# Attention over normalized images on one core: ten query sets that stay within a batch, four first tiles and two last ones transposed by TensorE, and the moves of a set shared by three DMA queues

## The chip, the cores and the metric

The kernel runs on one core of one Trainium2 chip. The metric is the device time in microseconds (us) of one execution; it is given as the median of several runs. An execution is also profiled once, and the trace of that execution is what the rows below are read from.

## What is computed

Four images x[b] of 128 channels by 1024 positions pass through one block of group norm, attention and projection, with a residual:

```
h = group_norm(x, 8 groups) * gn_w + gn_b
q = qw h + qb ; k = kw h + kb ; v = vw h + vb        # 128 x 1024 each
attn = softmax(q^T k / sqrt(128), axis=-1)           # 1024 x 1024 for each image
out = x + pw (v attn^T) + pb
```

All of it is float32.

## The kernel before

**Tiles and sets.** The 1024 queries of each of the 4 images are cut into 8 tiles of 128, so the program has 32 steps, numbered c = 0 to 31; b = c // 8 is the image ("batch") and i = c % 8 the tile in it. Step c makes the scores of tile c. The q and k weights are multiplied into one matrix beforehand (`g` is that product applied to h), and v carries the projection already. Scores are accurate products of float32 numbers split in a high and a low part (`h_hi`, `h_lo`, `g_hi`, `g_lo`): six matmuls of 512 columns a tile.

**What happens to one tile.** TensorE (PE) writes the scores into PSUM (`scores`). VectorE (DVE) copies them out with a bias and takes the row minimum (`drain_scores`, s_sb). ScalarE (ACT) takes the exponential and its sum (`exponentials`). The product with v needs the probabilities with keys on the partitions, that is transposed. For most tiles this is done in two parts: DVE transposes blocks of 32 x 32 (`transpose_blocks`, blocks), and DMA then moves the blocks from one group of 32 partitions to another (pT<-blocks). A set of four tiles is moved together, by 16 DMAs ("pieces") of 32 partitions x 4 KB: one for each source group a and destination group j. The first and the last two tiles are transposed by PE instead (`transpose_probs`, eight matmuls a tile into PSUM, copied out half by ACT and half by DVE, `copy_pair`). These are called direct.

**Sets.** `SETS = (2, 4, 4, 4, 4, 4, 4, 4, 2)`: set 0 and set 8 are direct, sets 1 to 7 are moved. Set 2 is tiles 6 to 9, so it lies half in image 0 and half in image 1; sets 4 and 6 cross an image in the same way. A set's product with v is done in units, one a tile, of eight matmul passes of 256 columns (`value_unit`). In a set within one image the units go by source groups: the first two need groups a = 0 and 1, that is the first 8 pieces, the last two the rest. In a set that crosses an image, each unit needs all 16 pieces.

**Order of work.** Every engine has one hand-written program, a loop over c, in order; engines wait for one another on semaphores. PE in step c does the scores of c, then the extra work of an image (`value_tiles`, `project_g` for the next image in steps with i = 6, 1, statistics), then the value unit of c - LAG, with LAG = 8. SP issues all DMAs but a few: `move_set(n)` waits until DVE has transposed the last tile of set n, which it does in step FIRST[n+1] (FIRST[n] is the first tile of set n), then issues the 16 pieces. GpSimd (POOL) computes the low part of h for the next image (`split_h`, i = 4), which the last matmul pass of `project_g` in steps 6, 14 and 22 reads, and adds the residual of finished sets. ACT also sends the inverse softmax sums of a set to a DRAM buffer (`copy_rows`, row_store), from where SP spreads them over all partitions (`spread_rows`, rden_bc<-row_store), so that DVE can divide (`divide`).

Of the kernel before, what the change touches and what calls it, by code (L numbers as in the profile page):

```python
# [22 lines left out]
LAG = 8  # L23


def build(nc, x, vectors, weights, out):
# [22 lines left out]
    with ExitStack() as ctx:  # L49
# [14 lines left out]
        def is_direct(c):  # L64
            return c < SETS[0] or c >= DIRECT

        def direct_number(c):
            return c if c < SETS[0] else c - DIRECT + SETS[0]

        def columns(n):  # L70

            return slice(P * FIRST[n], P * (FIRST[n] + SETS[n]))

        def last_batch(n):
            return (FIRST[n] + SETS[n] - 1) // CH

        def crosses(n):

            return FIRST[n] // CH != last_batch(n)

        def divided_in(c):

            for n in range(LS - 2):
                last = FIRST[n] + SETS[n] - 1
                if c == (FIRST_UNIT_STEPS[last] + 3 if n == 0 else last + LAG + 1):
                    return n
            return None
# [43 lines left out]
        pair_T = sb("pair_T", [P, KT, 2, P])  # L131
# [7 lines left out]
        sums = [ACC[:, n % 2, 0:P * SETS[n]] for n in range(LS)] + [S[:, 1, 0:PN]]  # L139
        last_sums = [ACC[:, (LS - 1) % 2, 0:UW], ACC[:, LS % 2, 0:UW]]  # L140
# [19 lines left out]
        MOVED = 16 * NQ  # L160
# [5 lines left out]
        normed_ready, last_normed, out_ready, tail_out_ready, stored = map(sem, ("normed_ready", "last_normed", "out_ready", "tail_out_ready", "stored"))  # L166
        tp_psum = sem("tp_psum")
        pair_ready = [sem(f"pair_ready{f}") for f in range(HALVES)]

        xb_flat = xb[:, :, :].rearrange("p b n -> p (b n)")  # L170
# [7 lines left out]

        block = ctx.enter_context(nc.Block())

        @block.sync
        def _(sp):
            def move_set(n):
                sp.wait_ge(blocks_ready, FIRST[n + 1] - SETS[0])
                if n > 2:
                    sp.wait_ge(part_done, FIRST[n - 1])
                for a in range(NQ):
                    for j in range(NQ):
                        sp.dma_start(moved_view(n)[Q * j:Q * (j + 1), a].rearrange("p t n -> p (t n)"),  # L189
                                     blocks_view(n)[Q * a:Q * (a + 1), j].rearrange("p t c q -> p (t c q)"))\  # L190
                          .then_inc(moved[n % 2][a], 16)
# [8 lines left out]
            def store_set(n):  # L200
                if n < SPREAD_BY_DMA:
                    sp.wait_ge(out_ready, n + 1)
                else:
                    sp.wait_ge(tail_out_ready, 2 if n == LS else 3)
                at = P * FIRST[n]
                while at < P * (FIRST[n] + SETS[n]):
                    b, first = at // N, at % N
                    width = min(N, first + P * (FIRST[n] + SETS[n]) - at) - first
                    sp.dma_start(out[b, :, first:first + width], xb[:, b, first:first + width]).then_inc(stored, 16)
                    at += width  # L210
# [20 lines left out]
            sp.wait_ge(stored, 16 * (NS + sum(crosses(n) for n in range(NS))))  # L231

        @block.tensor
        def _(pe):
            def group_deviations(b):
# [3 lines left out]
                if b > 1:  # L239
# [28 lines left out]
            def project_g(b, f):  # L268
# [598 lines left out]
```

## Time and profile before

| | us |
|---|---|
| median of 3 runs | 144.14 (143.91 to 144.76) |
| the profiled execution, its own time | 144.62 |
| its span, first to last instruction | 142.6 |
| PE busy | 130.1 |
| DVE busy | 99.5 |
| ACT busy | 64.9 |
| POOL busy | 26.1 |

The busy time of an engine counts computing instructions alone; the issuing of DMAs, as on SP, is not in it. The granted TensorE clock was full through the whole span.

### The profile page before, as it was taken

The numbers are of one execution on the slowest core, as the hardware profiler recorded it, in microseconds if no ns is written. First come the engines' busy times: TensorE is split into PE (matmuls) and PEld (weight loads), VectorE is DVE, ScalarE is ACT, GpSimd is POOL, SyncE is SP. The second block draws the span as 40 slices with busy tenths as digits, with TensorE's granted clock in tenths as the row PEclk, the third lists the DMA queues.
The fourth block names the chain that finished last, engine by engine and source line by source line (L and its number), as shares of the span: only waits on it lengthen the run. The fifth ranks groups of instructions, "written<-read, shape, count | busy, mean of one in ns | idle before, by whom it ended". The sixth has DMA issues, their size and how long they took to land.

```text
span 142.6 us, 2014 instructions
## 1 busy us (share of the span) xinstructions
PE 130.1 (91%) x647; PEld 109.4 (77%) x647; DVE 99.5 (70%) x172; ACT 64.9 (46%) x112; POOL 26.1 (18%) x33
## 2 busy tenths in 40 slices
PE   5999999997779999799999995999999969999990
PEld 5997878865558887688888883888888847988880
DVE  0577779989998679679697789366977893521222
ACT  4053789564566653544436845054543333512000
POOL 5043050930202061100050323000030030003000
PEclk9999999999999999999999999999999999999999
DMA  4950000005996799499824997899509987979211
GB/s 147 306 210 0 0 5 0 27 12 115 214 205 168 171 211 203 118 205 210 195 93 92 202 209 200 202 204 210 162 0 205 209 195 202 205 161 223 78 37 74
DMA packets 9565, 20.98 MB, mean 147 GB/s; under 512 B 2362, under 2 KB 4052, under 8 KB 9556
## 3 DMA queue, kind: packets, MB, share of 16 engines
q1 hardware_dynamic: 8816, 20.59, 59.3%
q10 hardware_dynamic: 740, 0.28, 0.7%
q8 instruction: 5, 0.08, 0.2%
q14 instruction: 4, 0.03, 0.1%
HBM read 4.07 MB, written 2.11 MB: 43 GB/s over the span
## 4 chain that ended last, share of the span: by engine, by line
PE 56%; SPq 19%; DVE 11%; issue 6%; DMA 5%; POOL 0%; DVEq 0%; POOLq 0%
PE ACC L377 20%; SPq L189 19%; PE S L322 6%; DMA pT<-blocks 5%; PE S L326 5%; PE S L323 5%; PE S L266 5%; DVE blocks L665 4%; DVE s_sb L656 4%; PE A L302 3%; PE ACC L350 2%; PE S L350 2%; PE A L404 1%; PE ACC L404 1%; DVE bn L581 1%
## 5 line engine op out<-in xcount | busy, mean ns | idle before, releaser
L377 PE MATMUL ACC<-pT,v 128*128 128x256 f32 x224 | 52.8, 381 | 4.1 <-DMA pT<-blocks 4.1
L656 DVE TENSOR_SCALAR_CACHE_REDUCE s_sb<-S,row_term 128x1024 f32<-128x1024 f32 x32 | 41.0, 1281 | 20.7 <-PE S L326 20.2
L377 PEld LDWEIGHTS ACC<-pT,v 128*128 128x128 f32 x224 | 41.2, 190 | 10.9 <-issue 5.6
L502 ACT ACTIVATE s_sb<-s_sb,rowmin 128x1024 f32<-128x1024 f32 x32 | 36.8, 1151 | 20.9 <-DVE s_sb L656 19.9
L665 DVE STREAM_TRANSPOSE blocks<-s_sb 128x1024 f32<-128x1024 f32 x28 | 34.7, 1240 | 0.0
L322 PE MATMUL S<-h_hi,g_hi 128*128 128x512 f32 x64 | 30.2, 472 | 0.3 <-issue 0.3
L323 PE MATMUL S<-h_lo,g_hi 128*128 128x512 f32 x64 | 25.2, 393 | 0.0
L326 PE MATMUL S<-h_hi,g_lo 128*128 128x512 f32 x64 | 19.9, 392 | 0.0
L810 POOL TENSOR_TENSOR xb<-rden_bc,xb 128x512 f32<-128x512 f32 (+1 forms) x7 | 8.4, 1194 | 53.0 <-DVE rden_bc L685 45.5
L326 PEld LDWEIGHTS S<-h_hi,g_lo 128*128 128x128 f32 x64 | 12.0, 188 | 2.8
L322 PEld LDWEIGHTS S<-h_hi,g_hi 128*128 128x128 f32 x64 | 12.1, 189 | 2.5 <-issue 0.4
L494 ACT COPY v<-A 128x384 f32<-128x384 f32 (+1 forms) x12 | 5.3, 443 | 18.8 <-PE A L302 18.8
L323 PEld LDWEIGHTS S<-h_lo,g_hi 128*128 128x128 f32 x64 | 12.1, 189 | 2.0
L302 PEld LDWEIGHTS A<-wpv,h 128*128 128x128 f32 x64 | 8.4, 191 | 3.7 <-issue 2.6
L302 PE MATMUL A<-wpv,h 128*128 128x129 f32 x64 | 9.5, 281 | 1.3 <-DVE g_lo L630 1.1
L797 POOL TENSOR_TENSOR h_lo<-h,h_hi 128x1024 fp32r<-128x1024 f32 x3 | 7.2, 2398 | 17.8 <-ACT h L472 17.8
L266 PE MATMUL S<-ident 128*128 128x128 f32 x38 | 7.9, 363 | 1.6 <-POOL ident L814 1.6
L482 ACT ACTIVATE g_hi<-A,wpv 128x512 fp32r<-128x512 f32 x7 | 4.8, 689 | 9.4 <-PE A L284 9.4
L266 PEld LDWEIGHTS S<-ident 128*128 128x128 f32 x38 | 6.9, 265 | 1.6 <-POOL ident L814 1.6
L788 POOL TENSOR_TENSOR rstd<-gvar,minus_half 128x1 f32<-128x1 f32 x4 | 2.2, 552 | 30.6 <-DVE gvar L603 30.6
L581 DVE BATCH_NORM_STATS2 bn<-x_sb 128x6 f32<-128x512 f32 x8 | 5.3, 683 | 2.9 <-DMA x_sb<-x 2.9
L467 ACT ACTIVATE h_hi<-x_sb,gshift,gscale 128x1024 fp32r<-128x1024 f32 (+1 forms) x5 | 5.2, 1067 | 2.1 <-DVE gshift L614 1.6
(90 smaller groups left out, 103.4 us busy)
## 6 DMA issues: line engine op xcount, KB each, us to landing
pT<-blocks SPq DMA_DIRECT2D x112, 128.0 KB, 2.4
rden_bc<-row_store SPq DMA_DIRECT2D x6, 256.0 KB, 3.6
x_sb<-x SPq DMA_DIRECT2D x1, 1024.0 KB, 6.0
out<-xb SPq DMA_DIRECT2D x8, 128.0 KB, 2.8
out<-xb SPq DMA_DIRECT2D x4, 256.0 KB, 3.2
x_sb<-x SPq DMA_DIRECT2D x2, 256.0 KB, 3.0
x_sb<-x SPq DMA_DIRECT2D x1, 512.0 KB, 3.9
w_in<-weights ACTq DMA_DIRECT2D x2, 128.0 KB, 3.5
```

The lines of the kernel that those rows point to most:

```text
L189: sp.dma_start(moved_view(n)[Q * j:Q * (j + 1), a].rearrange("p t n -> p (t n)"), blocks_view(n)[Q * a:Q * (a + 1), j].rearrange("p t c q ...
L266: pe.matmul(S[:, 0, BANK:BANK + P], ident[:, :], ident[:, :], start=True, stop=True)
L302: last = pe.matmul(A1[:, PW1 * u:PW1 * (u + 1)], h[:, P * t:P * (t + 1)], wpv[:, 0:PW1], start=True, stop=True)
L322: pe.matmul(S[:, c % 2, ks], g_hi[:, qs], h_hi[:, b % 2, ks], start=True, stop=False)
L323: pe.matmul(S[:, c % 2, ks], g_hi[:, qs], h_lo[:, b % 2, ks], start=False, stop=False)
L326: last = pe.matmul(S[:, c % 2, ks], g_lo[:, qs], h_hi[:, b % 2, ks], start=False, stop=True)
L377: last = pe.matmul(to, v[:, b % 3, t, :], probs[:, :, t, :], start=(t == 0), stop=(t == KT - 1))
L502: act.activation(s_sb[:, c % 3, :], s_sb[:, c % 3, :], ACT.Exp, bias=rowmin[:, c % CH:c % CH + 1], scale=-1.0, accum_out=den[:, n % 2, k:k ...
L656: dve.tensor_scalar(s_sb[:, c % 3, :], S[:, c % 2, :], row_term[:, b % 2, i:i + 1], None, ALU.add, ALU.min, accum_out=rowmin[:, i:i + 1]). ...
L665: dve.transpose(blocks_view(n)[:, :, :, k, :].rearrange("p j t q -> p t j q"), s_sb[:, c % 3, :].rearrange("p (t j q) -> p t j q", t=KT, j ...
L797: pool.tensor_tensor(h_lo[:, b % 2, :], h[:, :], h_hi[:, b % 2, :].bitcast(F32), ALU.subtract).then_inc(h_lo_ready, 1)
L810: pool.tensor_tensor(xs, rden_bc[:, n % 2, 0:P * SETS[n]], xs, ALU.add).then_inc(out_ready, 1)
```

## The change

- `SETS` becomes `(2, 2, 4, 4, 4, 4, 4, 4, 2, 2)`. Sets 0, 1 and 9 are direct (tiles 0 to 3 and 30, 31), sets 2 to 7 are moved sets of four tiles, and set 8 (tiles 28, 29) is a moved set of two. No set crosses an image. So two more tiles than before, 2 and 3, are transposed by PE.
- LAG becomes 7, and the units of tiles 0 to 3 run in steps 4 to 7; before, those of tiles 0 and 1 ran in steps 4 and 5, and those of tiles 2 and 3 in steps 10 and 11.
- Of the 16 pieces of sets 2 to 7, SP issues the 12 with j = 0 to 2 and POOL the 4 with j = 3, in step FIRST[n+1], ahead of `split_h`. Of the 16 pieces of set 8, which are half as long, SP issues 8 and ACT 8.
- The inverse sums are turned at i = 3 and 5 and copied by ACT at i = 4 and 6; SP's program takes `spread_rows(2)` ahead of `move_set(3)`, and after that each `spread_rows(n)` stands between `move_set(n)` and `move_set(n + 1)`.
- The last sets are finished without the halves that the set before last had.

The diff, cut to its core:

```diff
-SETS = (2, 4, 4, 4, 4, 4, 4, 4, 2)
-
-FIRST_UNIT_STEPS = (4, 5)
-LAG = 8
+SETS = (2, 2, 4, 4, 4, 4, 4, 4, 2, 2)
+PAIRS = 4
+
+FIRST_UNIT_STEPS = (4, 5, 6, 7)
+FIRST_DIVIDED_STEPS = (7, 9)
+LAG = 7
...
+        def move_piece(engine, n, a, j, counted):
+
+            engine.dma_start(moved_view(n)[Q * j:Q * (j + 1), a].rearrange("p t n -> p (t n)"),
+                             blocks_view(n)[Q * a:Q * (a + 1), j].rearrange("p t c q -> p (t c q)"))\
+                  .then_inc(counted[n % 2][a], 16)
...
             def move_set(n):
-                sp.wait_ge(blocks_ready, FIRST[n + 1] - SETS[0])
-                if n > 2:
+                sp.wait_ge(blocks_ready, FIRST[n + 1] - PAIRS)
+                if n > 3:
                     sp.wait_ge(part_done, FIRST[n - 1])
                 for a in range(NQ):
-                    for j in range(NQ):
...
+                    for j in range(NQ - 1 if n < LS - 1 else NQ // 2):
+                        move_piece(sp, n, a, j, moved)
...
             spread_rows(0)
-            move_set(1)
             spread_rows(1)
+            move_set(2)
             store_set(0)
-            for n in range(2, LS):
+            store_set(1)
+            spread_rows(2)
+            for n in range(3, LS):
                 move_set(n)
+                if n > 3:
+                    store_set(n - 2)
                 if n < SPREAD_BY_DMA:
                     spread_rows(n)
-                if n > 2:
-                    store_set(n - 2)
...
             def moved_unit(n, u):
-                b, part, half = (FIRST[n] + u) // CH, u // 2, u % 2
+                b, size = FIRST[n] // CH, SETS[n]
+                a0, width, half = (2 * (u // 2), 2, u % 2) if size == GC else (0, NQ, u)
...
+                    for a in range(a0, a0 + width):
+                        pe.wait_ge(moved[n % 2][a], MOVED * (n // 2) + (16 if n == LS - 1 else 0))
+                        if n < LS - 1:
+                            pe.wait_ge(keys_moved[n % 2][a], 16 * (n // 2))
...
-                if c - 1 in FIRST[1:LS]:
-                    turn_rden(FIRST.index(c - 1) - 1)
+                if i == 3 and (b == 0 or c > CH):
+                    turn_rden(2 * b if b > 0 else 0)
+                if i == 5:
+                    turn_rden(2 * b + 1)
...
             value_unit(STEPS - LAG)
+            value_unit(STEPS - LAG + 1)
             transpose_probs(STEPS - 1)
...
+            def move_last_set():
+                n = LS - 1
+                act.wait_ge(blocks_ready, DIRECT - PAIRS)
+                act.wait_ge(part_done, FIRST[n - 1])
+                for a in range(NQ):
+                    for j in range(NQ // 2, NQ):
+                        move_piece(act, n, a, j, moved)
...
                 exponentials(c)
+                if c == DIRECT:
+                    move_last_set()
...
+            def move_last_keys(n):
+                pool.wait_ge(blocks_ready, FIRST[n + 1] - PAIRS)
+                if n > 3:
+                    pool.wait_ge(part_done, FIRST[n - 1])
+                for a in range(NQ):
+                    move_piece(pool, n, a, NQ - 1, keys_moved)
...
                     add_bias((1, 3, 6, 7).index(c))
+                if c in FIRST[3:LS]:
+                    move_last_keys(FIRST.index(c) - 1)
                 if i == 4 and b < L:
                     split_h(b + 1)
```

Where this moves instructions is seen in the order of each engine's program.

First GpSimd, from the residual of set 0 (step 8 before, step 7 after) to that of set 2 (step 14 before, step 15 after). rstd and gscale are the group norm of the next image, h_lo is `split_h`. Before:

```order
L810 TENSOR_TENSOR xb<-rden_bc,xb 128x256
L788 TENSOR_TENSOR rstd<-gvar,minus_half 128x1
L790 TENSOR_TENSOR gscale<-rstd,cols 128x1
L797 TENSOR_TENSOR h_lo<-h,h_hi 128x1024
L810 TENSOR_TENSOR xb<-rden_bc,xb 128x512
```

After:

```order
L813 TENSOR_TENSOR xb<-rden_bc,xb 128x256
L174 DMA pT<-blocks 32x1024 x4
L813 TENSOR_TENSOR xb<-rden_bc,xb 128x256
L791 TENSOR_TENSOR rstd<-gvar,minus_half 128x1
L793 TENSOR_TENSOR gscale<-rstd,cols 128x1
L174 DMA pT<-blocks 32x1024 x4
L800 TENSOR_TENSOR h_lo<-h,h_hi 128x1024
L813 TENSOR_TENSOR xb<-rden_bc,xb 128x512
```

Four DMAs of set 2 stand in step 8 now, and four of set 3 in step 12, right ahead of h_lo; the same stands in step 20.

Second SP, from the loads of x on (rden_bc<-row_store is `spread_rows`, out<-xb a store). Before:

```order
L217 DMA x_sb<-x 128x2x1024
L197 DMA rden_bc<-row_store 128x256
L189 DMA pT<-blocks 32x1024 x16
L197 DMA rden_bc<-row_store 128x512
L209 DMA out<-xb 128x256
L189 DMA pT<-blocks 32x1024 x16
L197 DMA rden_bc<-row_store 128x512
```

After:

```order
L210 DMA x_sb<-x 128x2x1024
L194 DMA rden_bc<-row_store 128x256 x2
L174 DMA pT<-blocks 32x1024 x12
L203 DMA out<-xb 128x256 x2
L194 DMA rden_bc<-row_store 128x512
L174 DMA pT<-blocks 32x1024 x12
L194 DMA rden_bc<-row_store 128x512
```

A train has 12 pieces in place of 16, and the sums of set 2 are spread ahead of the moves of set 3.

Third PE, from the projection of g for image 1 in step 6 through step 7 (S is the scores, A<-wpv,h the value tiles, A<-ident,rden the turned sums). Before:

```order
L284 MATMUL A<-h_lo,wa_hi 128x512
L322 MATMUL S<-h_hi,g_hi 128x512
L323 MATMUL S<-h_lo,g_hi 128x512
L322 MATMUL S<-h_hi,g_hi 128x512
L323 MATMUL S<-h_lo,g_hi 128x512
L326 MATMUL S<-h_hi,g_lo 128x512 x2
L334 MATMUL A<-ident,rden 4x128
L302 MATMUL A<-wpv,h 128x129 x3
```

After:

```order
L283 MATMUL A<-h_lo,wa_hi 128x512
L358 MATMUL ACC<-pair_T,v 128x256 x4
L321 MATMUL S<-h_hi,g_hi 128x512
L322 MATMUL S<-h_lo,g_hi 128x512
L321 MATMUL S<-h_hi,g_hi 128x512
L322 MATMUL S<-h_lo,g_hi 128x512
L325 MATMUL S<-h_hi,g_lo 128x512 x2
L301 MATMUL A<-wpv,h 128x129 x3
L358 MATMUL ACC<-pair_T,v 128x256 x4
```

The units of tiles 2 and 3 (ACC<-pair_T,v) have come into steps 6 and 7, in which PE had none before.

## Rows read from the trace of the kernel before

**Rows 1.** The page: busy time, the chain by engine, and the group of drains.

```profile
PE 130.1 (91%) x647; PEld 109.4 (77%) x647; DVE 99.5 (70%) x172; ACT 64.9 (46%) x112; POOL 26.1 (18%) x33
...
PE 56%; SPq 19%; DVE 11%; issue 6%; DMA 5%; POOL 0%; DVEq 0%; POOLq 0%
...
L656 DVE TENSOR_SCALAR_CACHE_REDUCE s_sb<-S,row_term 128x1024 f32<-128x1024 f32 x32 | 41.0, 1281 | 20.7 <-PE S L326 20.2
```

**Rows 2.** Waits: engine, line, waited for; us in total, times, longest.

```profile
PE ACC L377 <- DMA pT<-blocks: 4.1, 3, 1.6
```

**Rows 3.** Timeline of PE: start, us, instruction, [idle before <-releaser].

```profile
56.62 0.39 PE L284 MATMUL A<-h_lo,wa_hi 128*128 128x512 f32 x1
57.94 1.97 PE L377 MATMUL ACC<-pT,v 128*128 128x256 f32 x8 [0.93 <-DMA pT<-blocks]
...
86.57 0.40 PE L284 MATMUL A<-h_lo,wa_hi 128*128 128x512 f32 x1
88.48 1.97 PE L377 MATMUL ACC<-pT,v 128*128 128x256 f32 x8 [1.52 <-DMA pT<-blocks]
...
115.69 0.61 PE L326 MATMUL S<-h_hi,g_lo 128*128 128x512 f32 x2
117.94 1.97 PE L377 MATMUL ACC<-pT,v 128*128 128x256 f32 x8 [1.64 <-DMA pT<-blocks]
```

**Rows 4.** The chain that ended last: start, us on the chain, what.

```profile
19.03 0.87 PE ACC L404 x8
...
22.28 0.23 PE S L322
...
23.67 1.73 PE ACC L350 x8
...
65.19 0.67 PE A L302 x6
...
128.23 0.66 PE S L340 x6
```

**Rows 5.** Timeline of PE, steps 6 to 12.

```profile
28.16 0.58 PE L322 MATMUL S<-h_hi,g_hi 128*128 128x512 f32 x1
...
45.13 0.58 PE L322 MATMUL S<-h_hi,g_hi 128*128 128x512 f32 x1
...
49.94 1.89 PE L377 MATMUL ACC<-pT,v 128*128 128x256 f32 x8
```

**Rows 6.** Timeline of DVE and of ACT, step 12.

```profile
51.34 1.24 DVE L665 STREAM_TRANSPOSE blocks<-s_sb 128x1024 f32<-128x1024 f32 x1
...
50.79 0.25 ACTq L511 DMA_DIRECT2D row_store<-rden_rows  x1
```

**Rows 7.** Timeline of POOL, step 12: split_h.

```profile
50.70 2.40 POOL L797 TENSOR_TENSOR h_lo<-h,h_hi 128x1024 fp32r<-128x1024 f32 x1 [6.82 <-ACT h L472]
```

**Rows 8.** Timeline of SP's queue.

```profile
45.37 10.55 SPq L189 DMA_DIRECT2D pT<-blocks  x16
56.04 0.51 SPq L197 DMA_DIRECT2D rden_bc<-row_store  x1
```

**Rows 9.** The chain, in the train of set 2: pieces issued.

```profile
45.92 1.11 SPq L189
47.08 0.59 SPq L189
47.71 0.59 SPq L189
```

**Rows 10.** The pieces of pT: from issue to landing.

```profile
DMA to landing us min/median/max: 2.3/2.4/4.1
```

**Rows 11.** Windows: us, engines, then granted clock, DMA share, GB/s.

```profile
49.00:56.00 7.00, 7.00 (x33) 5.93 (x32) 5.56 (x8) 4.25 (x8) 2.40 (x1) 1.00 0.94 206
...
2.00:6.00 4.00, 4.00 (x20) 3.91 (x20) 1.60 (x3) 1.22 (x2) 0.88 (x3) 1.00 0.93 287
```

**Rows 12.** Windows at the end: the store of the last set.

```profile
141.00:142.00 1.00, 0.00 (x0) 0.00 (x0) 0.00 (x0) 0.00 (x0) 0.00 (x0) 1.00 0.70 262
```

More of the change, by code:

```diff
@@ L64, in is_direct @@
         def is_direct(c):
-            return c < SETS[0] or c >= DIRECT
+            return c < PAIRS or c >= DIRECT
         def direct_number(c):
-            return c if c < SETS[0] else c - DIRECT + SETS[0]
+            return c if c < PAIRS else c - DIRECT + PAIRS
         def columns(n):
[L72 to L79, printed above, removed]
+            b, i = FIRST[n] // CH, FIRST[n] % CH
+            return b, slice(P * i, P * (i + SETS[n]))
         def divided_in(c):
-            for n in range(LS - 2):
-                last = FIRST[n] + SETS[n] - 1
-                if c == (FIRST_UNIT_STEPS[last] + 3 if n == 0 else last + LAG + 1):
+            for n in range(SPREAD_BY_DMA):
+                if c == (FIRST_DIVIDED_STEPS[n] if n < 2 else FIRST[n] + SETS[n] + LAG):
                     return n
@@ L137, in build @@
         A1 = psum("A1", [P, BANK])
-        sums = [ACC[:, n % 2, 0:P * SETS[n]] for n in range(LS)] + [S[:, 1, 0:PN]]
-        last_sums = [ACC[:, (LS - 1) % 2, 0:UW], ACC[:, LS % 2, 0:UW]]
+        sums = [A0[:, 0:PN]] + [ACC[:, n % 2, 0:P * SETS[n]] for n in range(1, LS)] + [S[:, 1, 0:PN]]
         PROD_V, PROD_ROW, PROD_G, PROD_C, PROD_B = 0, P, P + 1, P + 2, P + 3
@@ L159, in build @@
         moved = [[sem(f"moved{k}_{a}") for a in range(NQ)] for k in range(2)]
-        MOVED = 16 * NQ
+        keys_moved = [[sem(f"keys_moved{k}_{a}") for a in range(NQ)] for k in range(2)]
+        MOVED = 16 * (NQ - 1)
         part_done = sem("part_done")
@@ L203, in store_set @@
                 else:
[L204 to L210, printed above, removed]
+                    sp.wait_ge(tail_out_ready, 1 if n == LS else 2)
+                b, cs = columns(n)
+                sp.dma_start(out[b, :, cs], xb[:, b, cs]).then_inc(stored, 16)
             for f in range(HALVES):
@@ L230, in _ @@
             store_set(LS - 1)
-            sp.wait_ge(stored, 16 * (NS + sum(crosses(n) for n in range(NS))))
+            sp.wait_ge(stored, 16 * NS)
         @block.tensor
@@ L444, in _ @@
                     value_unit(FIRST_UNIT_STEPS.index(c))
-                if c >= LAG + SETS[0]:
+                if c >= LAG + PAIRS:
                     value_unit(c - LAG)
             value_unit(STEPS - LAG)
+            value_unit(STEPS - LAG + 1)
             transpose_probs(STEPS - 1)
-            for m in range(STEPS - LAG + 1, FIRST[LS - 1]):
+            for m in range(STEPS - LAG + 2, FIRST[LS - 1]):
                 value_unit(m)
@@ L555, in _ @@
                     normalize(b + 1)
-                if i == 4 and c - 2 in FIRST[1:LS]:
-                    copy_rows(FIRST.index(c - 2) - 1)
+                if i == 4:
+                    copy_rows(2 * b)
+                if i == 6:
+                    copy_rows(2 * b + 1)
                 if i == 6 and b < L:
@@ L561, in _ @@
                     copy_v(b + 1, 0)
-                if i == 7 and c - 1 in FIRST[1:LS]:
-                    copy_rows(FIRST.index(c - 1) - 1)
-                if c - 2 in range(SETS[0]):
+                if c - 2 in range(PAIRS):
                     copy_pair(c - 2)
@@ L747, in _ @@
                 drain_scores(c)
-                if c - 2 in range(SETS[0]):
+                if c - 2 in range(PAIRS):
                     copy_pair(c - 2)
```

126 lines of the change are left out of this document (57 added, 69 removed).

## The prediction

> **What bounds the kernel now.** I read the page first: PE is busy 130.1 of 142.6 us and leads the chain that ended last with 56%, but SP's queue holds 19% of it and DMA 5% [rows 1]. So PE is the bound, and it is held up somewhere by the moves. The list of waits names the place: three waits of the value units for pT [rows 2]. The timeline of PE then gives their size. After the last pass of `project_g` begins at 56.62 the next instruction could follow 0.23 us later, at 56.85; it starts at 57.94, so 1.09 us are lost. At 86.57 it is 88.48 - 86.81 = 1.67, and after the two passes at 115.69 (0.46 us) it is 117.94 - 116.15 = 1.79 [rows 3]. Together 4.55 us. All three are the first unit of sets 2, 4 and 6, those that cross an image and need all 16 pieces. The other sets need 8 pieces and never wait.
>
> The prices on PE come from the chain [rows 4]: eight transposes of a tile 0.87; the scores of a tile 23.67 - 22.28 = 1.39; a value unit 1.73; value tiles 0.67 (0.45 for the last two); six broadcasts of inverse sums 0.66. A plain step is 1.39 + 1.73 = 3.12. `project_g` is three passes, 0.70.
>
> A second loss is at the first image boundary. From the scores of step 6 (28.16) to those of step 11 (45.13) 16.97 us pass [rows 5]. The work in it is 5 x 1.39 + 2 x 0.70 + 0.67 + 0.67 + 0.45 + one unit 1.73 + 0.4 of small ones = 12.3. PE stands 4.7 us in it, waiting for DVE.
>
> **The change part by part.** The sum is made against the profiled span, 142.6, and carried over to the median 144.14 as a difference; the profiled execution itself took 144.62.
>
> *Transposes of tiles 2 and 3 on PE:* 2 x 0.87 = +1.74. They also save two block transposes on DVE, which is not the bound. *Broadcasts:* four for six at the end, -0.22.
>
> *Crossing sets gone:* the three waits go, -4.55.
>
> *Units 2 and 3 in steps 6 and 7:* they fill steps in which PE waited. I followed PE and DVE through steps 6 to 11 with the prices above, and for DVE 1.28 for a drain and 1.2 for a block transpose [rows 1, 6]. PE still waits about 0.6 us before `project_g` in step 9 and 1.5 before the value tiles in step 10, plus restarts, 2.5 in all where it was 4.7: -2.2. LAG 7 brings every later unit one step forward; it moves work and removes none.
>
> *Who issues, and what the DMA engines can do.* A piece leaves SP every 0.635 us (47.71 - 47.08, [rows 9]; 16 in 10.55, [rows 8]), which looks like a limit of SP. But within a train the DMA share is 0.94 at 206 GB/s [rows 11]. In the loads of x it is 0.93 too, at 287 GB/s, so I read a share near 1 as full engines. At a share of 1 a piece then takes 0.635 x 0.94 = 0.60 us, and four pieces from another queue come in between SP's and don't shorten the train by more than 6%. The Trainium skill says the same in "DMA: Bandwidth & Descriptors", Rules for kernel authors: spreading DMAs over SP, ACT and GpSimd doesn't raise bandwidth, it only saves the sequencer's issue time. By SP's issue time alone the six pieces that a first unit needs of SP would land 5 x 0.635 + 2.4 = 5.6 after the start [rows 9, 10]; by full engines ten pieces (POOL's four among them) are through 2.4 + 9 x 0.60 = 7.8 after it.
>
> What is on hand: with LAG 7 a first unit comes three steps after the step in which its last tile is transposed. For set 2 my walk gives blocks ready at 42.05 and PE at the unit at 48.05, so 6.0 against 7.8: a new wait of +1.8. (Lower end 0, by issue time alone.) For sets 3 and 5 it is a unit 1.73, a step with turned sums 3.23, one with `project_g` 3.82 and scores with value tiles 2.06, less the 2.5 from the end of the scores to the blocks (52.5 - 49.94, [rows 5, 6]), so about 8.3; for sets 4 and 6 about 9. Sets 3, 5 and 7 start late as well. SP now stands in `spread_rows(n - 1)` until ACT's row DMA, issued at 50.79 in step 12, has landed (at least 2.3 later, 53.1), then takes 0.51 to issue [rows 6, 8, 10]. That is 53.6 where DVE's blocks were ready at 52.5 [rows 6]. The spread itself is 256 KB, some 1.1 us of full engines. Ready after 7.8 + 1.1 = 8.9. For set 7, whose steps have no extra PE work, 7.9 is on hand: +1.0. For sets 3 and 5 the lateness of 0.6 disappears behind the next term.
>
> *POOL's four issues ahead of `split_h`.* In steps 12 and 20 POOL can issue only when DVE's blocks are ready (52.5 in step 12 of the trace), then does `split_h`, 2.40 [rows 6, 7]; before, it began at 50.70. The third pass of `project_g`, two steps later, needs its result and began at 56.62 [rows 3]. So 56.62 - 52.5 - 2.40 = 1.7 us are left for four issues, or 0.43 each. No row shows an issue by POOL. The bounds: 0.25, ACT's row DMA [rows 6], and 1.11, the longest of SP's in the chain of that train [rows 9]. I take 0.635, the same piece on SP, which is the nearest row. Then PE stands 4 x 0.635 - 1.7 = 0.84 twice: +1.7 (0 to 2 x 2.74 = 5.5). Behind the issues also stand POOL's residuals and the group scale of steps 9 and 10; those have 2 us and more to spare. The Trainium skill has "SWDGE first-byte ~1 us" against about 0.6 for the hardware queues (DMA: Bandwidth & Descriptors, Latency and other measured facts); if POOL were held for 1 us by each issue, which no row here shows, the estimate would be 2 x 2.3 = +4.6 in place of +1.7, and the time 146.4.
>
> *ACT's eight issues in step 30:* at 0.635 they hold ACT for 5.1 us, from 2.6 after the scores of step 30 to 7.7. Behind them stand the copy of tile 30 (0.6) and the exponential of tile 31 (1.3). PE reaches the transposes of tile 31 after unit 23, the scores of 31, 0.87 and three units, at 1.73 + 1.39 + 0.87 + 5.19 = 9.2; the probabilities are there at 9.6: +0.4 (0 at 0.25 an issue).
>
> *The last store* is half as long; 256 KB filled the slice from 141 to 142 to 0.70 [rows 12], so -0.3. The pieces of set 8 are ready more than 2 us before PE comes to them.
>
> Sum: 1.74 - 0.22 - 4.55 - 2.2 + 1.8 + 1.0 + 1.7 + 0.4 - 0.3 = -0.63. The span goes to 142.0, the median to **143.5**.
>
> **The rivals.** What can be told from no change in this kernel is about 0.5%, 0.7 us.
>
> *A. POOL's issues decide, and it is slower.* Place: `project_g` in steps 14 and 22. Each 0.1 us of an issue costs 0.8 us once it is over 0.43. At 0.71 the whole gain is gone; at the upper bound of 1.11 the sum grows by 8 x 0.475 = 3.8, and the time is 147.3. For it: POOL's own instructions are slow (2.40 for a subtraction of 1024 columns, [rows 7]), and no row says that it issues as fast as SP. Against it: the row on SP alone, for the same piece. Chance 0.36.
>
> *B. The DMA engines take the pieces in their stride.* Then the queues do what they look to do: no wait for set 2, none for set 7, 143.5 - 2.8 = 140.7, and with issues of 0.25 on POOL another 1.7 less, 139.0. For it: in before no unit waited that needed 8 pieces. Against it: the share of 0.94, with one queue alone. Chance 0.22.
>
> *C. The units of tiles 2 and 3 come at the wrong time.* They push the scores of steps 7 and 8 back, DVE gets its work later, and the boundary stays as long as it was: +2.2, 145.7. For it: the 4.7 us are waits for DVE, whose work there hardly shrinks. Against it: in my walk DVE never waits for the scores for more than 0.5 us in these steps. Chance 0.10.
>
> *The forecast* with issues of 0.55 to 0.75 on POOL and full engines, 142.8 to 144.5: chance 0.32.
>
> **How the numbers follow.** Faster by over 0.5% is under 143.4: nearly all of B (0.21), 0.4 of the forecast (0.13), a little of A, 0.01 of C, in all 0.36. Slower is over 144.9: most of A (0.32), C (0.09) and a rest of the forecast, in all 0.43. The rest is 0.21. The predicted time is the forecast's. The range leaves out the cheapest corner of B and the last of A: 140.0 to 147.2; the forecast's own range is 142.8 to 144.5.
>
> **What would show it.** The waits of PE for pT after steps with i = 6 and in step 31 should be gone, except at set 2's first unit (right if 1 to 2 us) and at set 7's (about 1). The DMA share in the trains should stand at 0.95 to 1.05, with pieces that land later than 2.4; if it rises well above 1 or the landings stay at 2.4, B is right. On POOL's timeline the gap from the end of the blocks of tiles 11 and 19 to h_lo, over four, is the price of an issue, and PE's gap before the third pass of `project_g` in steps 14 and 22 is that of A. In step 31 ACT's exponential should come some 5 us late and PE's transposes 0.4. The forecast is wrong first of all if an issue on POOL costs other than 0.6.

## The result

The changed kernel took 146.69 us (median of 4 runs, 146.36 to 148.92) where the kernel before, measured beside it, took 144.21: a ratio of 1.016, 95% interval 1.0116 to 1.0203. So it is slower, where the forecast of 143.5 had it a little faster; the time lies inside the stated range of 140.0 to 147.2 and outside the forecast's own. A later measurement of the same program, 10 runs of 144.15 to 149.77, gave a ratio of 1.0054 (1.0013 to 1.0096), with a median of 145.80 against 144.50; ratios leave out runs more than 1.5% above a kernel's fastest, medians do not, so where many runs of a kernel are long the ratio is the kinder figure. The two answers differ by more than their intervals, and much of what follows is about why the times of one program differ.

The page of the execution first profiled (148.92 us, clock 0.977), the parts that answer to [rows 1]:

```profile
span 147.2 us, 2087 instructions
...
PE 134.4 (91%) x662; PEld 113.0 (77%) x662; DVE 98.4 (67%) x172; ACT 65.7 (45%) x115; POOL 39.0 (27%) x58
...
PEclk9999999999999857999999999999999999999999
...
PE 60%; SPq 11%; DMA 11%; issue 7%; DVE 5%; POOL 3%; ACT 1%; DVEq 0%; POOLq 0%
...
L174 POOL DMA_DIRECT2D pT<-blocks x24 | 12.1, 511 | 42.5 <-DVE blocks L679 42.5
...
pT<-blocks SPq DMA_DIRECT2D x72, 128.0 KB, 3.6
pT<-blocks POOLq DMA_DIRECT2D x24, 128.0 KB, 4.6
```

The transposes of two more tiles, less two broadcasts, would make PE's busy time 1.5 longer; it grew by 4.3. The row of the clock says why to look further: in slices 14 to 16 it isn't whole. SP's pieces now land after 3.6 us where they took 2.4 [rows 10].

PE's timeline of the same execution (start, us, instruction, [idle before <- what ended it]), every stop of more than 0.4 us behind step 11, and the unit behind the first of them:

```profile
51.22 3.75 PE L379 MATMUL ACC<-pT,v 128*128 128x256 f32 x8 [3.37 <-DMA pT<-blocks]
57.28 1.89 PE L379 MATMUL ACC<-pT,v 128*128 128x256 f32 x8
64.72 0.50 PE L283 MATMUL A<-h_lo,wa_hi 128*128 128x512 f32 x1 [0.47 <-POOL h_lo L800]
94.19 0.50 PE L283 MATMUL A<-h_lo,wa_hi 128*128 128x512 f32 x1 [0.45 <-POOL h_lo L800]
98.95 1.97 PE L379 MATMUL ACC<-pT,v 128*128 128x256 f32 x8 [0.48 <-DMA pT<-blocks]
127.97 3.69 PE L379 MATMUL ACC<-pT,v 128*128 128x256 f32 x16 [1.00 <-DMA pT<-blocks]
132.07 1.97 PE L379 MATMUL ACC<-pT,v 128*128 128x256 f32 x8 [0.41 <-DMA pT<-blocks]
```

The stops in the crossing sets [rows 3] are gone, as the forecast said. In their place PE stands 3.5 us ahead of set 2's first unit, from 47.7 on (a stand is idle time of PE ahead of an instruction), and the unit then takes 3.75 in place of 1.97. The windows over that place (length, five engines, then granted clock, DMA share, GB/s):

```profile
46.00:48.00 2.00, 1.84 (x11) 1.20 (x9) 2.00 (x5) 1.56 (x3) 0.40 (x2) 1.00 0.93 277
48.00:50.00 2.00, 0.00 (x0) 0.00 (x0) 2.00 (x5) 1.81 (x3) 0.00 (x0) 1.00 0.84 213
50.00:52.00 2.00, 0.79 (x2) 0.73 (x3) 0.52 (x1) 1.91 (x4) 0.00 (x0) 0.60 0.88 201
52.00:54.00 2.00, 2.00 (x6) 1.55 (x6) 0.00 (x0) 0.00 (x0) 0.00 (x0) 0.50 0.76 206
54.00:56.00 2.00, 2.00 (x6) 1.58 (x5) 0.00 (x0) 0.00 (x0) 0.00 (x0) 0.50 0.31 103
56.00:58.00 2.00, 2.00 (x8) 1.63 (x7) 0.52 (x1) 0.00 (x0) 0.00 (x0) 0.70 0.09 28
```

PE does nothing for over 3 us, the granted clock falls to 0.50 of full speed (1.2 of 2.4 GHz, the lower of its two levels), and with PE at work it is whole again from 58 on. From the start of that unit to the start of the next are 57.28 - 51.22 = 6.06 us. In a profile where the clock stayed whole the same stretch is 3.19 (below), so the half clock costs 2.9 in this execution. The Trainium skill ("TensorE: Matmul & The Clock Gate", Part 1: The HAM clock gate) says that the half clock is the engine's idle state and that activity releases it. These windows agree: a fall behind 3.5 us without work, a rise with PE busy. The prediction had not weighed it.

### The profile page after: what moved, and what is told of

It reads as the page before. It is cut to its first block, busy times and chain, and to the rows that moved or that the text cites. A ratio compares the mean times of both kernels' runs of the same rounds, so it can differ in the third digit from the quotient of the medians.

```text
span 147.2 us, 2087 instructions
## 1 busy us (share of the span) xinstructions
PE 134.4 (91%) x662; PEld 113.0 (77%) x662; DVE 98.4 (67%) x172; ACT 65.7 (45%) x115; POOL 39.0 (27%) x58
## 4 chain that ended last, share of the span: by engine, by line
PE 60%; SPq 11%; DMA 11%; issue 7%; DVE 5%; POOL 3%; ACT 1%; DVEq 0%; POOLq 0%
PE ACC L379 19%; SPq L174 11%; DMA pT<-blocks 9%; PE S L321 7%; PE S L322 6%; PE S L325 6%; PE S L263 5%; PE A L301 3%; DVE blocks L679 2%; PE ACC L406 2%; PE A L358 2%; PE S L358 2%; POOL h_lo L800 2%; DMA row_store<-rden_rows 1%; DVE s_sb L669 1%
## 5 line engine op out<-in xcount | busy, mean ns | idle before, releaser
L379 PE MATMUL ACC<-pT,v 128*128 128x256 f32 x208 | 51.1, 392 | 5.3 <-DMA pT<-blocks 5.3
L379 PEld LDWEIGHTS ACC<-pT,v 128*128 128x128 f32 x208 | 39.5, 196 | 12.2 <-issue 6.7
L679 DVE STREAM_TRANSPOSE blocks<-s_sb 128x1024 f32<-128x1024 f32 x26 | 32.3, 1241 | 0.0
L321 PE MATMUL S<-h_hi,g_hi 128*128 128x512 f32 x64 | 31.0, 485 | 0.3 <-issue 0.3
L322 PE MATMUL S<-h_lo,g_hi 128*128 128x512 f32 x64 | 25.7, 401 | 0.0
L174 POOL DMA_DIRECT2D pT<-blocks x24 | 12.1, 511 | 42.5 <-DVE blocks L679 42.5
L813 POOL TENSOR_TENSOR xb<-rden_bc,xb 128x512 f32<-128x512 f32 (+1 forms) x8 | 9.1, 1136 | 35.9 <-DVE rden_bc L699 30.4
L325 PEld LDWEIGHTS S<-h_hi,g_lo 128*128 128x128 f32 x64 | 12.3, 192 | 3.0
L699 DVE TENSOR_TENSOR rden_bc<-ACC,rden_bc 128x512 f32<-128x512 f32 (+1 forms) x7 | 4.5, 647 | 3.7 <-PE ACC L379 3.6
```

The source lines that it names most:

```text
L174: engine.dma_start(moved_view(n)[Q * j:Q * (j + 1), a].rearrange("p t n -> p (t n)"), blocks_view(n)[Q * a:Q * (a + 1), j].rearrange("p t ...
L321: pe.matmul(S[:, c % 2, ks], g_hi[:, qs], h_hi[:, b % 2, ks], start=True, stop=False)
L322: pe.matmul(S[:, c % 2, ks], g_hi[:, qs], h_lo[:, b % 2, ks], start=False, stop=False)
L325: last = pe.matmul(S[:, c % 2, ks], g_lo[:, qs], h_hi[:, b % 2, ks], start=False, stop=True)
L379: last = pe.matmul(to, v[:, b % 3, t, :], moved_view(n)[:, a0:a0 + width, t, :], start=(t == 0), stop=(t == KT - 1))
L679: dve.transpose(blocks_view(n)[:, :, :, k, :].rearrange("p j t q -> p t j q"), s_sb[:, c % 3, :].rearrange("p (t j q) -> p t j q", t=KT, j ...
```

## The experiments

Twelve experiments ran, the first of them the changed kernel again. 1 to 4, 5 to 8, 9 to 11 and 12 were measured together, each group beside its own runs of the kernel before; its medians were 144.50, 144.54, 144.55 and 144.31. "Clock under 0.99" counts the runs whose mean granted clock says that it was halved somewhere; it was so in none of the 58 runs of the kernel before. In the changed kernel's first measurement it was so in 4 of 4.

**1. The changed kernel again.** No edit.

> The changed kernel once more, unchanged, beside the others. Theory 1 (the stand of PE ahead of the first unit of set 2 is what made the change slow, and the half clock behind it doubles the price): PE stands about 3.5 us from 47.7 on, and the granted clock falls to half in some microseconds around it; the time is 146.4 to 146.8. Theory 2 (POOL's issues ahead of split_h are the loss): two gaps of 0.6 us ahead of the third pass of project_g, as in the profile after, which would be 1.2 us of a loss of 2.3. If the clock stays whole this time, theory 1 loses its second half.

Measured: 145.80 median, clock under 0.99 in 4 of 10 runs. The profile caught a run with a whole clock, span 143.6 us. PE's timeline:

```profile
50.36 1.96 PE L379 MATMUL ACC<-pT,v 128*128 128x256 f32 x8 [2.66 <-DMA pT<-blocks]
53.55 1.89 PE L379 MATMUL ACC<-pT,v 128*128 128x256 f32 x8
```

The same wait, 0.7 shorter and with no fall behind it: 3.6 us of span lie between two executions of one program. So the place was as theory 1 had it, but not the size, and in this run its second half did not show: a stand of 2.66 can pass without a fall. The median is 0.6 under the 146.4 to 146.8 expected. Theory 2's two stops ahead of `project_g`'s third pass are there in both profiles, so they don't make the difference. Of the seven fastest runs two at 0.988 took 146.2 on the mean and five at a whole clock 144.9, so the fall that such a run has costs 1.3. The clock isn't all: the slowest of the ten, 149.77, had a whole clock. No profile caught such a run, and what held it up stays open.

**2. SP issues all pieces.** POOL's four pieces go back to SP's queue, behind SP's own of the same quarter `a`.

```diff
                     for j in range(NQ - 1 if n < LS - 1 else NQ // 2):
                         move_piece(sp, n, a, j, moved)
+                    if n < LS - 1:
+                        move_piece(sp, n, a, NQ - 1, keys_moved)
...
-                if c in FIRST[3:LS]:
-                    move_last_keys(FIRST.index(c) - 1)
```

> SP issues all 16 pieces of sets 2 to 7 again, POOL none; everything else as changed. Theory 1: with one queue the eight pieces of the first unit of set 2 land 7 x 0.635 + 0.5 + 2.4 = 7.3 us after the blocks at about 42, so at 49.3; the stand is 1.6 us in place of 3.5 and the clock stays whole; the two gaps ahead of project_g go as well. 146.6 - 1.9 - 1.5 to 2.9 (clock) - 1.2 = 140.6 to 142.0. If instead the sharing with POOL helps (the rival that the queues are the limit), the first units wait longer than now and the time is 147 or more.

Measured: 147.04 median, far from the 140.6 to 142.0 of theory 1 and as its rival had it: 143.88 in the profiled run (span 141.9, clock whole), then 146.68, 147.40 and 148.51 with clocks of 0.977 to 0.988. The profile, the train and the two stops:

```profile
41.94 10.12 SPq L174 DMA_DIRECT2D pT<-blocks  x16
...
49.01 1.97 PE L381 MATMUL ACC<-pT,v 128*128 128x256 f32 x8 [1.08 <-DMA pT<-blocks]
...
126.75 1.97 PE L381 MATMUL ACC<-pT,v 128*128 128x256 f32 x8 [2.92 <-DMA pT<-blocks]
```

With everything on one queue the first unit has its 8 pieces (a = 0 and 1) 7.07 us after SP's first issue; with four pieces on POOL it was 51.22 - 41.85 = 9.37 and 50.36 - 41.74 = 8.62. With the second queue the first unit came later, so the rival's number came true without its reason: the stops ahead of `project_g` and most of set 2's stand went. The second queue helps the end of a train, which is what set 7 waits for: its stand is 2.92 now, which the expectation had not counted, and the clock falls in three runs of four. Where it falls in them no profile shows.

**3. PE kept busy ahead of set 2's first unit.** 30 matmuls of `ident` by itself, into sums that the unit starts anew.

```diff
+            def keep_busy(n):
+                for _ in range(n):
+                    pe.matmul(ACC[:, 0, 384:512], ident[:, :], ident[:, :], start=True, stop=True)
...
+                if c == LAG + PAIRS:
+                    keep_busy(30)
                 if c >= LAG + PAIRS:
                     value_unit(c - LAG)
```

> The changed kernel with 30 idle matmuls of 128 x 128 (0.11 us each, 3.3 us) put ahead of the first unit of set 2, into a bank that this unit overwrites. PE waits as long as before but does not stand. Theory 1: the unit still starts at about 51.2, but the granted clock stays whole, so the steps behind it have their usual 3.1 us: faster than the changed kernel by 1.5 to 2.9 us, 143.7 to 145.1. If the clock has nothing to do with the stand, nothing changes: 146.4 to 146.8.

Measured: 149.09 median, ratio 1.0314 (1.0262 to 1.0366), clock 0.998 or more in all four runs. The expected 143.7 to 145.1 was missed by its own price: I had taken a matmul for 0.11 us; each shows as two records, 0.23 us together:

```profile
47.91 6.86 PE L267 MATMUL ACC<-ident 128*128 128x128 f32 x60
```

So the filler lasted 3.4 us too long for a price. The clock held, but the test had to be made again.

**4. The units of tiles 4 to 7 one step later.** Two units come in step 15, and the division of set 2 moves one step as well (left out of the lines below).

```diff
-                if c >= LAG + PAIRS:
+                if c in (12, 13, 14, 15):
+                    value_unit(c - LAG - 1)
+                if c > 14:
                     value_unit(c - LAG)
```

> The changed kernel with the units of set 2 one step later (tiles 4 to 7 in steps 12 to 15, that of tile 8 in step 15 too) and the division of set 2 one step later. PE does the scores of step 12 (1.4 us) ahead of the first unit, and the blocks are unchanged. Theory 1: the stand is 3.5 - 1.4 = 2.1 us, nothing is lost later, the clock stays whole: 146.6 - 1.4 - 1.5 to 2.9 = 142.3 to 143.7. If the moves are late by their own contention and not by LAG, only 1.4 us or less come back: 145.2.

Measured: 143.87 (143.22 to 144.18), ratio 0.9939 (0.9914 to 0.9963), clock 0.997 or more in all seven; the median is 0.2 above the expected 142.3 to 143.7. The stand is 1.89 (at 51.08), not 3.4, and no clock is lost: this one move turned a loss into a gain of 0.6%.

**5. The filler at its right length,** 15 matmuls.

> 15 matmuls of ident by ident (128 columns) stand ahead of set 2's first value unit; the run with 30 showed that each takes 0.223 us, so 15 take 3.35 us and end at about 51.2 us, where the unit began at 50.4 to 51.2 without them. Theory (it is PE's idle time ahead of that unit that halves the granted clock, and the half clock that makes the same kernel take 146 to 148 in some runs): clock 0.997 or more in all runs, span 143.8 to 144.6, median 145.3 to 146.0 with a spread under 1 us. Rival (the clock falls for another reason, as a state of the chip): the clock is 0.98 to 0.99 in about half of the runs, as in the changed kernel, and the median is 146.3 or more.

Measured: 146.67, clock 0.997 or more in five of six runs; ratio 1.0134 (1.0112 to 1.0156). The filler ended at about 51.6, and PE's unit followed at once. Five runs had spans of 144.3 to 145.1, and the median is 0.7 above the expected end: by the time alone the rival would have it (146.3 or more), by the clock the theory does. The sixth, the profiled one, had a fall elsewhere: PE stood ahead of set 5's first unit. Its timeline and windows:

```profile
98.23 2.94 PE L383 MATMUL ACC<-pT,v 128*128 128x256 f32 x8 [2.23 <-DMA pT<-blocks]
```

```profile
96.00:98.00 2.00, 0.00 (x1) 0.00 (x0) 1.93 (x4) 1.72 (x3) 0.01 (x1) 1.00 1.07 232
98.00:100.00 2.00, 1.77 (x6) 1.54 (x7) 0.00 (x0) 0.00 (x0) 0.00 (x0) 0.77 0.89 272
100.00:102.00 2.00, 2.00 (x6) 1.55 (x6) 0.00 (x0) 0.00 (x0) 0.00 (x0) 0.50 0.17 64
```

The fall goes with a stand of PE, not with one place in the program. The median is 0.9 above experiment 1's, though the clock held: the filler makes PE's unit come at 51.6 in every run where it came at 50.36 in that profile, and the rest isn't explained.

**6. Late units, and POOL's issues behind `split_h`.**

```diff
-                if c in FIRST[3:LS]:
-                    move_last_keys(FIRST.index(c) - 1)
                 if i == 4 and b < L:
                     split_h(b + 1)
+                if c in FIRST[3:LS]:
+                    move_last_keys(FIRST.index(c) - 1)
```

> The units of tiles 4 to 7 one step later, as in the run before (141.5 span, 143.87 median), and in steps 12 and 20 POOL issues its four pieces behind split_h. Theory (the issues hold h_lo back by 4 x 0.50 us): the stop of 0.45 before the third pass of project_g goes, 0.6 us; POOL's pieces of sets 3 and 5 land 2.4 later, which is just in time: span 140.9, median 143.3. Rival: the later pieces hold up the first units of sets 3 and 5 by as much as was won: span 141.5, and the list of waits shows them for DMA.

Measured: 143.78, ratio 0.9926 (0.9899 to 0.9954), which can't be told from experiment 4; the clock was under 0.99 in two of nine runs, and a third long one (145.22) had it whole. The rival was right (span 142.0). The stops at `project_g` went, and set 5's first unit waits for the later pieces:

```profile
54.94 2.01 POOL L174 DMA_DIRECT2D pT<-blocks  x4
...
93.91 1.96 PE L379 MATMUL ACC<-pT,v 128*128 128x256 f32 x8 [1.13 <-DMA pT<-blocks]
```

**7. Late units, and SP issues all pieces:** the edits of 2 and 4 together.

> Units of tiles 4 to 7 one step later, and SP issues all pieces. Theory (POOL's pieces slow SP's own; by one queue alone the first unit of set 2 had its 8 pieces 7.2 us after the start, by two only after 8.6 to 9.2): set 2's first unit comes at 49.2 with no wait, no stop before the third pass of project_g, but set 7's second half waits 2.9 us as in the kernel where SP issues all: span 140.5 where the clock stays whole. If a stand of PE is what halves the clock, the one of 2.9 us near 124 does it, in many runs: clock 0.98 to 0.99, times 143 to 146. Rival (the pieces land late because the DMA engines are full): set 2's first unit waits as with two queues, 1.5 us or more, span 141.5 or more.

Measured: 147.76, from 144.38 to 150.18, above the expected 143 to 146; clock under 0.99 in three of six, and one at a whole clock took 149.33. The profile (span 143.7) has set 2's unit at 50.05, 7.68 after the first issue with a stop of 0.31, and set 7's second half:

```profile
128.60 1.97 PE L381 MATMUL ACC<-pT,v 128*128 128x256 f32 x8 [3.31 <-DMA pT<-blocks]
```

The clock is whole in this profile in spite of 3.31: not every stand of that size brings a fall. The span was 3.2 above what I expected; set 3's first unit waited too (1.15 at 64.23), behind a train of 16.

**8. Late units, and POOL issues for set 7 alone,** where the end of the train matters and POOL holds up nothing. SP issues the other sets' (POOL's pieces get semaphores of their own, left out here).

```diff
+                    if n < LS - 2:
+                        move_piece(sp, n, a, NQ - 1, keys_moved)
...
-                if c in FIRST[3:LS]:
-                    move_last_keys(FIRST.index(c) - 1)
+                if c == FIRST[LS - 1]:
+                    move_last_keys(LS - 2)
```

> Units of tiles 4 to 7 one step later; SP issues all 16 pieces of sets 2 to 6, and POOL four of set 7's alone. Theory: no stand of over 1 us anywhere behind step 12, so the clock is whole in all runs; set 7 waits 1.3 to 1.9 as with two queues: span 139.0 to 139.8, median 141.0 to 141.8, which beats both kernels. Rival (late pieces by full engines): no better than the kernel with late units, 143.5 to 144.

Measured: 143.06, ratio 0.9908 (0.9881 to 0.9935), span 141.0, clock 0.996 or more in all six. No stand is over 1 us and the clock held, as expected, but the gain is smaller: 141.0 to 141.8 was expected and 143.5 to 144 by the rival, so the time lies between. Set 3's first unit waited 0.98, where it waited 1.15 in 7.

**9. Two of POOL's four pieces go back to SP.** POOL keeps those of a = 0 and 1, which the first unit needs; SP takes the others in their turn. This tells apart what slows the first unit: a second queue as such, or the two pieces for the second half that POOL puts ahead of it.

```diff
                     for j in range(NQ - 1 if n < LS - 1 else NQ // 2):
                         move_piece(sp, n, a, j, moved)
+                    if n < LS - 1 and a >= NQ // 2:
+                        move_piece(sp, n, a, NQ - 1, keys_moved)
...
-                for a in range(NQ):
+                for a in range(NQ // 2):
                     move_piece(pool, n, a, NQ - 1, keys_moved)
```

> POOL issues only two of its four pieces of each moved set, those that the first unit needs (a = 0, 1); SP issues the other two behind its own of the same a. Theory (the DMA engines serve both queues side by side, so POOL's two pieces for the second half stand ahead of SP's for the first): the first unit of set 2 now waits for 8 pieces and not for 10 and starts 7.0 to 7.7 us after SP's first issue, as with one queue, in place of 8.3 to 9.4; the stand is 1 to 1.5 us. The stops before the third pass of project_g (0.6 twice) go too, since POOL is held for 1.0 and not for 2.0. Span 143.6 - 1.3 - 1.2 = 141.1 where the clock stays whole, median 143 to 143.5. Rival (a second queue slows the first as such, by arbitration): the first unit still starts 8.5 us or more behind the first issue, span 142.4 or more.

Measured, the timelines of SP's queue, of POOL and of PE:

```profile
42.41 10.00 SPq L174 DMA_DIRECT2D pT<-blocks  x14
42.70 1.22 POOL L174 DMA_DIRECT2D pT<-blocks  x2 [6.27 <-DVE blocks L681]
...
49.73 1.97 PE L381 MATMUL ACC<-pT,v 128*128 128x256 f32 x8 [1.32 <-DMA pT<-blocks]
...
126.79 3.53 PE L381 MATMUL ACC<-pT,v 128*128 128x256 f32 x8 [2.77 <-DMA pT<-blocks]
```

The first unit starts 49.73 - 42.41 = 7.32 us behind the first issue, inside the 7.0 to 7.7 of the theory; with four pieces on POOL it took 8.3 to 9.4 in four profiles. (In 10 and 12, with the same two pieces on POOL, PE came to the unit 7.31 and 7.22 behind the first issue, and the timelines show no wait.) There is no stop at `project_g`. The chain of this profile, from SP's fourth issue on, says more:

```profile
44.32 1.70 SPq L174
...
46.06 0.64 SPq L174
...
46.75 2.74 DMA pT<-blocks
```

That fourth issue is long with two pieces on POOL (1.70) as with four (1.55 to 1.79 in four profiles), and takes 0.59 where POOL issues none (2 and 11). So beside a second queue SP's issues do slow down, by about as much as the two issues that it saves SP here. What is gone is the late landing: SP's last piece for the unit lands 2.74 after its issue, where it took 3.19 to 4.97 with four pieces on POOL and 2.5 with none. The unit was late by the two pieces that POOL put ahead of it, and not by a second queue as such; whether their order or their number counts this edit doesn't tell. (The Trainium skill, "DMA: Bandwidth & Descriptors", Issuing engines are not separate DMA queues, says that transfers of all issuing engines interleave on the same DMA engines; the profile agrees, with 7.3 against 8.3 and more.) But the time did not follow: 145.47 (143.26 to 148.6) against 144.55, where 143 to 143.5 was expected; the ratio of 0.9972 (0.9929 to 1.0014) compares six of the 12 runs, and the clock was under 0.99 in 8 of 12. The trains of 14 are late at their end, and PE stands 2.77 ahead of set 7's second half. The windows:

```profile
124.00:126.00 2.00, 0.02 (x1) 0.00 (x0) 0.00 (x0) 0.84 (x2) 0.00 (x0) 1.00 1.02 212
126.00:128.00 2.00, 1.21 (x3) 1.06 (x4) 0.17 (x1) 0.89 (x2) 0.00 (x0) 0.64 0.99 309
128.00:130.00 2.00, 2.00 (x6) 1.53 (x6) 0.00 (x0) 0.00 (x0) 0.00 (x0) 0.51 0.58 131
```

The second half's first unit takes 3.53 in place of 1.97. From its start to the next transposes are 130.15 - 126.79 = 3.36 us, where they are 1.80 in 10's profile with a whole clock: this fall, in a run of mean clock 0.988, costs 1.6.

**10. The same with late units:** the edits of 4 and 9.

> The same with the units of tiles 4 to 7 one step later. Theory: the first unit of set 2 comes without a wait (it is on hand 7.4 us after SP's first issue), set 7's pieces come as with two queues: span 139.5 to 140.5, median 141.5 to 142.5, the clock whole in all runs. Rival (arbitration): as the kernel with late units alone, 143.3 to 144.

Measured: 143.54 (142.05 to 148.1), ratio 0.9893 (0.9848 to 0.9937), clock under 0.99 in three of six. Set 2's unit has no wait, but the expected 141.5 to 142.5 and the whole clock did not come: PE stands 2.84 ahead of set 7's second half, in a profile of 141.5 with a whole clock. The median is the rival's, its reason is not: the pieces of set 2 were there in time.

**11. The edit of 8 without late units.**

> The changed kernel with SP issuing all pieces of sets 2 to 6 and POOL four of set 7's alone; units as in the changed kernel. The kernel where SP issues all 16 of set 7 too had a stand of 2.9 us ahead of set 7's second half and clock 0.977 to 0.988 in most runs. Theory (that stand is what halved its clock; set 2's of 1 us does not): clock whole in nearly all runs, set 2's first unit stands 1 to 2 us, set 7's waits fall to 1.5 to 2: span 140.8 to 141.6, median 142.7 to 143.7. Rival (the stand at set 2 halves the clock here too): clock 0.988 in half of the runs, median over 144.5.

Measured: 143.64, inside the expected 142.7 to 143.7, ratio 0.9919 (0.9891 to 0.9948), span 141.7, clock under 0.99 in two of seven. Set 2's unit came 7.06 after the first issue with a stop of 1.06, set 7's stops were 0.21 and 1.26.

**12. Late units, two pieces on POOL in sets 2 to 6, all four in set 7.** (The lines of experiment 4 and the new semaphores are left out.)

```diff
+                    if n < LS - 2 and a >= NQ // 2:
+                        move_piece(sp, n, a, NQ - 1, keys_moved)
...
-                for a in range(NQ):
-                    move_piece(pool, n, a, NQ - 1, keys_moved)
+                for a in range(NQ // 2 if n < LS - 2 else NQ):
+                    move_piece(pool, n, a, NQ - 1, keys_moved if n < LS - 2 else pool_moved)
```

> As the kernel with two pieces on POOL and late units (141.5 span, a stand of 2.84 ahead of set 7's second half, clock 0.988 in half of the runs, median 143.54), but POOL issues all four pieces of set 7. Theory (set 7's wait comes from SP's longer train there; the stand behind it is what halves the clock now): set 7's waits fall from 2.84 to 1.2 to 1.6 in sum, the clock is whole in all runs, span 139.8 to 140.6, median 141.5 to 142.5, spread under 1.5 us. Rival (the clock falls whatever set 7 does): clock 0.988 in two runs of six or more, median 143.5.

Measured: 142.18 (141.43 to 142.42), ratio 0.9833 (0.9809 to 0.9858), clock 0.996 or more in all six runs, span 140.4, all as expected. It beats both kernels. The page, and then PE's timeline:

```profile
PE 131.9 (94%) x662; PEld 111.6 (79%) x662; DVE 98.1 (70%) x172; ACT 65.8 (47%) x115; POOL 34.3 (24%) x48
...
PE 73%; DVE 9%; issue 7%; SPq 6%; DMA 2%; POOL 0%; ACT 0%; DVEq 0%; POOLq 0%
```

```profile
49.81 1.96 PE L384 MATMUL ACC<-pT,v 128*128 128x256 f32 x8
...
92.78 1.97 PE L384 MATMUL ACC<-pT,v 128*128 128x256 f32 x8 [0.56 <-ACT v L504]
...
125.30 1.96 PE L384 MATMUL ACC<-pT,v 128*128 128x256 f32 x8 [0.63 <-DMA pT<-blocks]
```

SP and DMA hold 8% of the chain that ended last, where it was 24% before [rows 1] and 22% in the changed kernel.

## Why the prediction was wrong

**Where it held.** The three waits of the crossing sets went (-4.55). At the first boundary the scores of steps 6 and 11 start at 29.87 and 46.09, 16.22 us apart in place of 16.97 [rows 5], with one unit (1.73) more between them: the work between is 12.3 + 1.73 = 14.0, so PE stands 2.2 where it stood 4.7: -2.5 where I wrote -2.2, and rival C is out. The walk gave set 2's start as 42.05 and PE at its unit as 48.05; they were 41.85 and 47.7. Rival A had the right place and sign: `project_g` stops twice, 0.63 and 0.60 us. But four issues on POOL took 1.97 to 2.18, about 0.50 each, against my 0.635: +1.2 in place of +1.7. (By my own formula 0.50 would have given 8 x 0.07 = 0.6; POOL's room was smaller than I read.) A did not decide, and the sign that I put first, a price of an issue on POOL other than 0.6, was not what made the forecast wrong. Nor did B decide: the units of sets 2 and 7 did wait.

**The step that failed** is "the new wait of +1.8" for set 2, and what I left out behind it. I set the landing of the tenth piece at 7.8 us after the start, from a piece every 0.60 us and 2.4 to land. The first unit started 8.3 to 9.4 after it in the four profiles with this queueing, 8.9 on the mean. The chain of the profile of 147.2 us shows where the time went:

```profile
43.13 0.59 SPq L174
43.72 0.04 issue
43.76 1.56 SPq L174
45.32 0.04 issue
45.37 0.59 SPq L174
45.96 0.04 issue
46.00 4.97 DMA pT<-blocks
```

One issue takes 1.56, and the piece issued at 46.00 lands 4.97 later, where I took the median of 2.4 from a single queue [rows 10]. (A long issue alone isn't the second queue's mark: 1.11 in [rows 9] and one of 1.65 in 8 stand in trains of one queue.) The kind of step was right, ten pieces and not eight: when POOL's two pieces for the second half aren't ahead (2, 7, 8, 9, 11) the unit starts after 7.07, 7.68, 8.08, 7.32 and 7.06, 7.4 on the mean. Its size was too small, because I carried a landing time over from a queue that ran alone. The wait of +1.8 measured 3.5 in this profile and 2.8 in that of experiment 1.

The second half of the failure is a term that isn't in the sum at all: a stand of this size can halve PE's clock. In the profiled run it cost 2.9, in runs of a mean clock of 0.988 about 1.3 (experiment 1). The evidence, with the longest stand of PE on moves behind step 11 in each kernel's one profile:

| | longest stand | runs with a clock under 0.99 | median |
|---|---|---|---|
| changed kernel, first | 3.37 | 4 of 4 | 146.69 |
| 7 | 3.31 | 3 of 6 | 147.76 |
| 2 | 2.92 | 3 of 4 | 147.04 |
| 10 | 2.84 | 3 of 6 | 143.54 |
| 9 | 2.77 | 8 of 12 | 145.47 |
| 1, the same kernel | 2.66 | 4 of 10 | 145.80 |
| 5 | 2.23 | 1 of 6 | 146.67 |
| 4 | 1.89 | 0 of 7 | 143.87 |
| 11 | 1.26 | 2 of 7 | 143.64 |
| 6 | 1.20 | 2 of 9 | 143.78 |
| 8 | 0.98 | 0 of 6 | 143.06 |
| 3 | 0.87 | 0 of 4 | 149.09 |
| 12 | 0.63 | 0 of 6 | 142.18 |

That is 26 of 48 runs in the upper seven rows and 4 of 39 in the lower six; the line between them was drawn afterwards. With the stand filled (3, 5) or shortened and nothing else changed (4), the clock was under 0.99 in one run of 17, and that fall lay at another stand; with the stand as it was, in 8 of 14. In all three profiles with a fall it begins at a stand, of 3.37, 2.23 and 2.77; but 2.66, 2.84, 2.92 and 3.31 passed without one. That the stand brings the fall is shown; what decides between two executions of one program stays open, and for the four falls of 6 and 11, which no profile caught, so does the place. Nor does the clock explain every long run: three (149.77 in 1, 149.33 in 7, 145.22 in 6) had it whole.

**The smaller terms.** Set 5's first unit lost 0.6 (I had 0). Set 7 lost 1.8 in two stops (I had 1.0). ACT's eight issues took 5.60 and made its exponential late as described, but PE itself was late by set 7's wait, so the 0.4 was nothing. The sum by measured terms is -0.63 - 0.3 (first boundary) + 1.7 (set 2) + 2.9 (clock) - 0.5 (POOL) + 0.6 (set 5) + 0.8 (set 7) - 0.4 (ACT) = +4.2, against 147.2 - 142.6 = +4.6 in the two profiles; 0.4 stays unassigned. For the profile of 143.6 in experiment 1 the stand of 2.8 adds 1.0 in place of 1.7, set 7 lost 2.0 in place of 1.8 and the clock nothing: +0.8, against +1.0. With the 1.3 of a run at 0.988 that is +2.1 to +2.3, near the +2.5 of the first medians. So even with a whole clock the change doesn't pay.

## What to carry to other kernels

Give a second queue only pieces that are wanted as soon as the first queue's: with two pieces for later ahead of it, the piece that PE stood for landed after 3.2 to 5.0 us here, and after 2.7 without them. Price a new wait not only by its length: behind stands like those here (2.2 to 3.4 us in the three profiles with a fall) the half clock can cost 1.3 to 2.9 more, in some executions and not in others, so put other work ahead of the wait. Take many runs of a kernel that has such a wait before believing a verdict: here one program measured +1.6% and +0.5%.

## What the runs showed of the hardware

- For a stretch two queues moved more than one at about the same DMA share: it was 0.93 at 277 GB/s with two queues (46 to 48, above; 213 at 0.84 in the next 2 us), and 0.94 at 206 with one [rows 11]. The share near 1 that I read as full engines is no limit of bytes; the 287 GB/s at 0.93 in the same rows said so already. SP's own issues slow down meanwhile: 12 in 9.64 us, 0.80 each, where 16 took 10.55 [rows 8]. The Trainium skill's rule that spreading DMAs over queues doesn't raise bandwidth ("DMA: Bandwidth & Descriptors", Rules for kernel authors) isn't what this row shows, though over the whole train the gain is small.
- An issue of a piece on POOL holds it about 0.50 us (the page's mean is 511 ns), less than the 0.59 to 0.60 of an issue on SP, and a piece issued there lands 4.6 later at the median, on SP's queue beside it 3.6.
- A matmul of 128 by 128 in f32 shows as two records: 30 of them as 60, in 6.86 us. A transpose of the same size is one, eight in 0.87 [rows 4].
- PE's granted clock can fall to half inside a busy kernel, behind stands of 2.2 to 3.4 us, and is back with PE at work; one fall cost 2.9 us and one 1.6.
